# Two transformer layers in one kernel: router logits bank by bank, the last feed-forward's weights combined after the first expert's matmuls, the second attention's head rows gathered into one contraction, its last two matmul layers one bank apart

## The reference, cut to what matters

```
1 attention   16 heads of 64, causal, q/k/v from wq wk wv, output projection wo
2 mixture     8 experts, top 2 of softmax(x @ router_w + router_b), capacity 640 tokens
              per expert; gelu(x @ w1 + b1) @ w2 + b2, weighted sum
3 attention   16 heads of 8 with rotary positions, causal, scores equal to 0 masked too,
              output @ wo.T
4 feed-forward  h = x @ (w_fc as -1/0/1 times its scale).T + gate * x @ v.T @ fast_b.T @ u.T
              y = relu(h)^2 @ (w_proj as -1/0/1 times its scale).T
```

## Time and profile before

| | us |
|---|---|
| median of 3 runs | 1240.81 |
| lowest and highest of them | 1238.11, 1241.08 |
| the profiled execution's own time | 1239.13 |
| its span in the profile | 1237.3 |
| PE busy in the span | 1121.1 (91%) |
| PE weight loads, DVE, ACT, POOL busy | 851.2, 862.2, 815.4, 349.4 |
| mean granted TensorE clock | 0.958 of full |

### The profile page before, as it was taken

How to read it: one execution, slowest core, us unless ns; L and a number is a source line. 1 busy time by engine, 2 the same in 40 slices (tenths; PEclk the granted TensorE clock), 3 DMA queues, 4 the chain that set the end, 5 groups by cost and what they waited for, 6 DMA issues and landing times.

```text
span 1237.3 us, 28186 instructions
## 1 busy us (share of the span) xinstructions
PE 1121.1 (91%) x10202; PEld 851.2 (69%) x10202; DVE 862.2 (70%) x2486; ACT 815.4 (66%) x1915; POOL 349.4 (28%) x345
## 2 busy tenths in 40 slices
PE   5999999999999999999899976987888888888886
PEld 3787878787888787888576653665566556556674
DVE  6656566565656565645334547999999899999863
ACT  3766666767666666631233434998889889989932
POOL 1974646455464646213001202000000000000043
PEclk8999999999999999999599995998999899999998
DMA  6222223222322323211011043020310202110001
GB/s 161 59 69 76 69 58 77 63 59 64 80 54 70 76 59 75 65 36 34 15 35 43 25 97 46 2 40 27 66 31 10 40 6 36 26 15 2 2 1 34
DMA packets 33627, 58.90 MB, mean 48 GB/s; under 512 B 4906, under 2 KB 18114, under 8 KB 33490
## 3 DMA queue, kind: packets, MB, share of 16 engines
q1 hardware_dynamic: 32690, 55.52, 19.9%
q10 hardware_dynamic: 800, 1.57, 0.4%
HBM read 27.59 MB, written 4.33 MB: 26 GB/s over the span
## 4 chain that ended last, share of the span: by engine, by line
PE 56%; DVE 18%; issue 11%; ACT 7%; POOL 5%; DMA 2%; SPq 1%; ACTq 0%; POOLq 0%; DVEq 0%
PE pT L1278 12%; PE pO L1201 12%; PE pS L1239 10%; DVE Zb L956 9%; PE pS L1352 4%; ACT probs L719 3%; PE pT L1149 3%; PE pT L1365 3%; DVE Sm L971 3%; PE pS L1313 2%; PE pT L1153 2%; PE pS L1430 1%; ACT PT L699 1%; PE pS L1410 1%; DMA KS<-split 1%
## 5 line engine op out<-in xcount | busy, mean ns | idle before, releaser
L1278 PE MATMUL pT<-cst,probs 128*128 128x128 f32 x2304 | 369.9, 287 | 53.4 <-ACT probs L719 49.2
L1278 PEld LDWEIGHTS pT<-cst,probs 128*128 128x128 f32 x2304 | 257.0, 143 | 149.0 <-ACT probs L719 99.7
L719 ACT ACTIVATE probs<-probs,nmax 128x128 f32<-128x128 f32 (+7 forms) x256 | 198.7, 776 | 129.9 <-DVE nmax L966 128.9
L699 ACT COPY PT<-pT 128x512 f32<-128x512 f32 (+3 forms) x576 | 263.9, 482 | 16.8 <-PE pT L1278 15.6
L966 DVE CUSTOM_DVE_ANT_0 probs<-pS,causal_wide 128x128 f32<-128x128 f32 (+7 forms) x256 | 192.0, 750 | 91.2 <-PE pS L1239 83.6
L719 ACT ACTIVATE probs<-Sm,nmax 128x128 f32<-128x128 f32 (+7 forms) x256 | 199.6, 780 | 55.4 <-DVE nmax L971 49.1
L1201 PE MATMUL pO<-PT,V 128*64 128x128 f32 (+1 forms) x4608 | 233.5, 281 | 2.5 <-DVE attnT L925 1.1
L956 DVE TENSOR_SCALAR Zb<-pS 128x128 bf16<-128x128 f32 (+7 forms) x256 | 192.7, 753 | 20.0 <-PE pS L1245 19.4
L1201 PEld LDWEIGHTS pO<-PT,V 128*64 128x64 f32 (+1 forms) x4608 | 180.9, 114 | 36.3 <-issue 21.0
L971 DVE CUSTOM_DVE_ANT_0 Sm<-pS,Zb 128x128 f32<-128x128 f32 (+7 forms) x256 | 193.3, 755 | 4.5
L543 POOL TENSOR_TENSOR rstd<-rstd,power 128x4 f32<-128x4 f32 x32 | 32.6, 1019 | 552.4 <-DVE rstd L824 552.4
(11 more groups left out here) (189 smaller groups left out, 1370.2 us busy)
## 6 DMA issues: line engine op xcount, KB each, us to landing
wq_t<-factors SPq DMA_DIRECT2D x32, 256.0 KB, 4.0
Qs<-Ql SPq DMA_DIRECT2D x30, 256.0 KB, 3.7
Kh<-Kh SPq DMA_DIRECT2D x30, 256.0 KB, 3.4
Kl<-Kl SPq DMA_DIRECT2D x30, 256.0 KB, 4.6
QS<-split SPq DMA_DIRECT2D x72, 64.0 KB
KS<-split SPq DMA_DIRECT2D x72, 64.0 KB
w1s<-in_w SPq DMA_DIRECT2D x16, 128.0 KB, 2.3
w2s<-in_w SPq DMA_DIRECT2D x16, 128.0 KB, 2.2
```

Of the source, the lines that this page charges most:

```text
L699: nc.scalar.copy(PT[:, g % 2, h, k0 * P:(k0 + nk) * P], pT[r % TBANKS][:, 0:nk * P])\
L719: nc.scalar.activation(probs[:, i % NPROB, 0:n], src[:, 0:n], ACT.Exp, bias=nmax[:, i % 4:i % 4 + 1], scale=-1.0, accum_out=total).then_in ...
L1278: m = nc.tensor.transpose(pT[r % TBANKS][:, kt * P:(kt + 1) * P], probs[:, item % NPROB, (k0 + kt) * P:(k0 + kt + 1) * P], ident)
```

## The change

- In the stretch before the router the weight combination is gone. PE goes through the banks: transposes of bank j, then the logit matmuls of bank j-1 behind the copy of that bank alone.
- The weight combination stands behind `up(0)` and ahead of the rank counts, in banks 7 and 6, and ACT's three copies stand behind the first expert's gelus. PE waits for the last two of these copies ahead of the ninth transpose of the router weights.
- SP gathers the four heads of each half of the second attention by four transfers (8 partitions x 4 KB, SBUF to SBUF) into `compact[P, B, S]`, where head n lies on partitions 8n to 8n+7. The gather of half i stands behind the stacks of half i+2 in SP's order, and the last two behind the loop; each waits until its half's outputs are written. The output projection is one contraction per tile, and PE waits for a batch's 16 transfers ahead of that batch's first tile. `wo1s` is the plain transposed weight.
- The fourth sublayer's normalised input has a buffer of its own, `xn3`, since `compact` lies where `xn` was.
- In the last layers PE does bank j's upper matmuls ahead of bank j-1's projection.

The buffers, and SP's gathers:

```diff
-        wo1s = at(130, "wo1s", [P, G1, D])
+        wo1s = at(130, "wo1s", [P, D])
+        compact = at(148, "compact", [P, B, S])
+        xn3 = at(64, "xn3", [P, NT, D])
...
+            def gather(half):
+                b, g = divmod(half, G1)
+                sp.wait_ge(A[1]["n"], (half + 1) * ST)
+                for h in range(HPG):
+                    row = (g * HPG + h) * DH1
+                    sp.dma_start(compact[row:row + DH1, b, :], attn1T[h * (P // HPG):h * (P // HPG) + DH1, b, g, :])\
+                        .then_inc(ld_compact[b], 16)
...
                 if half == 2:
                     store(2)
                     store(3)
+                gather(half - 2)
+            gather(G1 * B - 2)
+            gather(G1 * B - 1)
```

On ScalarE, and on TensorE ahead of the router and behind `up(0)`:

```diff
-            act.wait_ge(lowA_done, 1)
-            nc.scalar.activation(lowA[:, :], bank[4][0:RANK, 0:D], ACT.Copy, scale=gates[:, 0:1]).then_inc(lowA_ready, 1)
-            act.wait_ge(w1e_done, 1)
-            nc.scalar.copy(w1e[:, :], bank[5]).then_inc(we_ready, 1)
-            act.wait_ge(w2e_done, 1)
-            nc.scalar.copy(w2e[:, :, :], bank[6]).then_inc(we_ready, 1)
             copies_T(1)
...
             gelus(0)
+            act.wait_ge(lowA_done, 1)
+            nc.scalar.activation(lowA[:, :], bank[7][0:RANK, 0:D], ACT.Copy, scale=gates[:, 0:1]).then_inc(lowA_ready, 1)
+            act.wait_ge(w2e_done, 1)
+            nc.scalar.copy(w2e[:, :, :], bank[6]).then_inc(we_ready, 1)
+            act.wait_ge(w1e_done, 1)
+            nc.scalar.copy(w1e[:, :], bank[7]).then_inc(we_ready, 1)
...
-            nc.tensor.matmul(bank[4][0:RANK, 0:D], fbs[:, :], vs[:, :], start=True, stop=True).then_inc(lowA_done, 1)
...
-            m.then_inc(w1e_done, 1)
-            pe.wait_ge(we_ready, 2)
-            transposes(1)
             pe.wait_ge(zeros_ready, 3)
-            pe.wait_ge(xnT_ready[1], NB)
-            for n in range(NT):
-                nc.tensor.matmul(bank[4][:, n * E:(n + 1) * E], xnT[:, n * P:(n + 1) * P], rws[:, :],
-                                 start=(n == 0), stop=False, skip_group_check=True)
+            for j in range(NB + 1):
+                if j < NB:
+                    pe.wait_ge(xn_ready[1], j + 1)
+                    for t in range(TPB):
+                        i = nc.tensor.transpose(bank[4 + j][:, t * P:(t + 1) * P], xn[:, j * TPB + t, :], ident)
+                    i.then_inc(tr_done[1], 1)
+                if j >= 1:
+                    pe.wait_ge(xnT_ready[1], j)
+                    for n in range((j - 1) * TPB, j * TPB):
+                        nc.tensor.matmul(bank[4][:, n * E:(n + 1) * E], xnT[:, n * P:(n + 1) * P], rws[:, :],
+                                         start=(n == 0), stop=False, skip_group_check=True)
...
             up(0)
+            nc.tensor.matmul(bank[7][0:RANK, 0:D], fbs[:, :], vs[:, :], start=True, stop=True).then_inc(lowA_done, 1)
+            pe.wait_ge(q_p, 5 * (FC1 + 1))
+            for f in range(FC1):
+                m = nc.tensor.transpose(bank[6][:, f * P:(f + 1) * P], wpj[:, f * P:(f + 1) * P], ident)
+            m.then_inc(w2e_done, 1)
+            pe.wait_ge(lowA_ready, 1)
+            for f in range(FC1):
+                nc.tensor.matmul(bank[7][:, f * P:(f + 1) * P], lowA[:, :], uTs[:, f * P:(f + 1) * P], start=True, stop=False)
+                m = nc.tensor.matmul(bank[7][:, f * P:(f + 1) * P], wfc[:, f, :], ident, start=False, stop=True)
+            m.then_inc(w1e_done, 1)
             pe.wait_ge(r_, 8 + NT)
...
             for n in range(NT):
+                if n == 2 * TPB:
+                    pe.wait_ge(we_ready, 2)
                 m = nc.tensor.transpose(bank[4 + n // TPB][0:E, (n % TPB) * P:(n % TPB + 1) * P], wgt[:, n, :], ident)
```

On TensorE in the second attention's output projection and the last layers:

```diff
             for n in range(NT):
-                for g in range(G1):
-                    m = nc.tensor.matmul(bank[n // TPB][:, (n % TPB) * P:(n % TPB + 1) * P],
-                                         attn1T[:, n // ST, g, (n % ST) * P:(n % ST + 1) * P], wo1s[:, g, :],
-                                         start=(g == 0), stop=(g == G1 - 1))
+                if n % ST == 0:
+                    pe.wait_ge(ld_compact[n // ST], 16 * HEADS)
+                m = nc.tensor.matmul(bank[n // TPB][:, (n % TPB) * P:(n % TPB + 1) * P],
+                                     compact[:, n // ST, (n % ST) * P:(n % ST + 1) * P], wo1s[:, :], start=True, stop=True)
...
                     m.then_inc(tr_done[3], 1)
+                    pe.wait_ge(xnT_ready[3], j + 1)
+                    for f in range(FC1):
+                        u = j * FC1 + f
+                        if u >= 2:
+                            pe.wait_ge(relu_ready, u - 1)
+                        nc.tensor.matmul(bank[6 + f % 2], w1e[:, f * P:(f + 1) * P], xnT[:, j * BANK:(j + 1) * BANK],
+                                         start=True, stop=True).then_inc(fc_done, 1)
                 if j >= 1:
                     pe.wait_ge(sq_ready, j * FC1)
...
-                if j < NB:
-                    pe.wait_ge(xnT_ready[3], j + 1)
...
```

More of the change, by code:

```diff
@@ L342, in build @@
         ld_stack = [sem("ld_stack0"), sem("ld_stack1")]
+        ld_compact = [sem("ld_compact0"), sem("ld_compact1")]
         lg_done = sem("lg_done")
@@ L473, in _ @@
             sp.wait_ge(y_done[1], NB)
-            sp.dma_start(wo1s[:, :, :], wo1).then_inc(ld_wo1, 16)
+            sp.dma_start(wo1s[:, :], wo1).then_inc(ld_wo1, 16)
             sp.wait_ge(tr_done[1], NB)
@@ L850, in norm_stage @@
                     if what == "x norm":
-                        norm(k, 1, j, lambda n: X[:, n, :], lambda n: xn[:, n, :], xn_ready[k])
+                        to = xn3 if k == 3 else xn
+                        norm(k, 1, j, lambda n: X[:, n, :], lambda n: to[:, n, :], xn_ready[k])
             def y_tile(n):
@@ L1322, in _ @@
                 pe.wait_ge(A[0]["cp_" + e2], L[0].copied[e2])
-            nc.tensor.matmul(bank[4][0:RANK, 0:D], fbs[:, :], vs[:, :], start=True, stop=True).then_inc(lowA_done, 1)
[L1324 to L1331, removed]
-            m.then_inc(w1e_done, 1)
-            pe.wait_ge(we_ready, 2)
-            transposes(1)
-            pe.wait_ge(zeros_ready, 3)
-            pe.wait_ge(xnT_ready[1], NB)
-            for n in range(NT):
-                nc.tensor.matmul(bank[4][:, n * E:(n + 1) * E], xnT[:, n * P:(n + 1) * P], rws[:, :],
-                                 start=(n == 0), stop=False, skip_group_check=True)
+            pe.wait_ge(zeros_ready, 3)
+            for j in range(NB + 1):
[9 more added lines that the diff above has]
+                                         start=(n == 0), stop=False, skip_group_check=True)
             nc.tensor.matmul(bank[4][:, 0:NT * E], onesf[:, :], rbs[:, :].rearrange("o (n e) -> o n e", n=1).to_broadcast([1, NT, E]),
@@ L1422, in _ @@
                     for t in range(TPB):
-                        m = nc.tensor.transpose(bank[4 + j % 2][:, t * P:(t + 1) * P], xn[:, j * TPB + t, :], ident)
+                        m = nc.tensor.transpose(bank[4 + j % 2][:, t * P:(t + 1) * P], xn3[:, j * TPB + t, :], ident)
                     m.then_inc(tr_done[3], 1)
+                    pe.wait_ge(xnT_ready[3], j + 1)
[5 more added lines that the diff above has]
+                                         start=True, stop=True).then_inc(fc_done, 1)
                 if j >= 1:
@@ L1432, in _ @@
                     m.then_inc(y_done[4], 1)
-                if j < NB:
-                    pe.wait_ge(xnT_ready[3], j + 1)
[L1435 to L1438, removed]
-                        nc.tensor.matmul(bank[6 + f % 2], w1e[:, f * P:(f + 1) * P], xnT[:, j * BANK:(j + 1) * BANK],
-                                         start=True, stop=True).then_inc(fc_done, 1)
 def kernel(L0_attn_x, L0_attn_wq, L0_attn_wk, L0_attn_wv, L0_attn_wo, L0_ffn_router_w, L0_ffn_router_b, L0_ffn_w1,
@@ L1454 @@
     wl1 = np.stack([qkv[0], qkv[0][:, swap], qkv[1], qkv[1][:, swap], qkv[2]]).reshape(5, D, D).transpose(2, 0, 1)
-    wo1 = np.zeros((HPG, P // HPG, G1, D), np.asarray(L1_attn_wo).dtype)
-    wo1[:, 0:DH1] = np.asarray(L1_attn_wo).T.reshape(G1, HPG, DH1, D).transpose(1, 2, 0, 3)
     arrays = {
```

2 lines of the change are left out of this document (1 added, 1 removed).

## The result

| | before | after |
|---|---|---|
| median of 4 runs each, us | 1239.46 (1237.72 to 1241.08) | 1226.50 (1225.86 to 1227.89) |
| profiled execution, its span | 1239.13, 1237.3 | 1227.89, 1226.1 |
| PE busy | 1121.1 | 1103.0 |
| mean granted clock | 0.958 | 0.961 |

The ratio is 0.990 (95% interval 0.988 to 0.992), a gain clear of the noise though small. The forecast of 1232.0 had the sign and the two places right; the time lies under the low end of the range, 1228.

What follows compares the result with a forecast made beforehand. The kernel was taken as a row of stages with separate limits, its last-ending chain more than half PE. Router 2.4 plus tail 6.4 made 8.8 us, taking 1240.8 to 1232.0; overall range 1228 to 1237.

Steps and rivals of the forecast that it cites:

- logits by bank: Before the router: logits follow each bank's copy, so DVE starts the router at 587.7, 3.6 us earlier.
- rank counts behind the combination: Router: the counts wait for the moved combination on PE, losing 1.2 us of the 3.6 gained.
- router weights and b2: Router, 602.03 to 612.65: assumed to keep its 10.6 us, so no gain.
- start of up(1) to the first down: Start of the experts: instructions unchanged, so no gain counted.
- stages that don't change, second attention above all: First attention, experts, second attention: same instructions, so they only shift; no gain counted.
- tail: After the second attention: last statistics 7.8 us earlier, less 1.4 for a low clock, leaving 6.4 us.
- Part 1: Before the router: combination moved away and logits done bank by bank; DVE starts at 587.7, 3.6 us earlier.
- Part 2: Combination behind up(0), ending 598.3 at full clock: counts wait 1.2 us, leaving 2.4 us gained.
- Part 3 and 4: Gather with shorter projection, 2.73 us; last layers 8.6 us a bank instead of 9.3; together 7.8, or 6.4 with low clock.
- The rival that ends slower: Last layers: clock stays low after the wait at 1180 to 1184.9, 13.1 us a bank; total 1247; chance 5%.
- The rival on a better clock: No fall at 1184.9, counts undelayed, b2 products at 0.114: up to 14.9 us gained, 1225.9; chance 10%.
- they move as a block: First attention, experts and second attention keep their instructions, so they only shift in time; no gain counted.

Runs made afterwards that it cites:

- e2_tail: Kernel before with the change's gather, compact, xn3, plain wo1s and last-layer order, router as before; 1231.70 us, ratio 0.9947.
- e4_early: Changed kernel with the weight combination put back ahead of the banked transposes and logits; 1228.66 us, ratio 0.9931.
- e3: Kernel before with only the new order of the last layers, bank j's upper matmuls ahead of bank j-1's projection; 1235.89 us, ratio 0.9990.
- e11_att: e9_fillAB with the first score product doubled for items of up to three key tiles in the second attention; 1225.77 us.
- e12_before: Kernel before, unchanged, profiled again; 1240.70 us in one run.
- e16_after: Changed kernel, unchanged, profiled again; 1224.65 us in one run.
- e7_fill: Changed kernel with useless matmuls in three PE waits: five before the router's last xn, ten before the second attention, five before the last layers' first xn; 1226.35 us.
- e9_fillAB: Changed kernel with useless matmuls in two PE waits: five before the router's last xn, five before the last layers' first xn; 1225.06 us.
- e13_fill3: e9_fillAB with three more useless matmuls before the weight combination's second half; 1225.28 us.
- e8_gather: Kernel before with gather, compact, xn3 and the single contraction, last layers in the old order, router as before; 1234.29 us, ratio 0.9958.

## Why the prediction was right or wrong

By terms, forecast against the means of the profiles (tail and unchanged stages: four of each kernel; router: seven with the old code, five with the new):

| term | forecast | measured |
|---|---|---|
| logits by bank | 3.6 | 3.4 (18.0 to 14.66) |
| rank counts behind the combination | -1.2 | -0.5 (0 to -0.9) |
| router weights and b2 | 0 | 1.2 (8.4 to 7.25); 3.0 in the first pair |
| start of up(1) to the first down | 0 | -0.2 |
| stages that don't change, second attention above all | 0 | 2.0, not told from chance |
| tail | 6.4 | 6.2; 5.6 in the first pair |
| sum | 8.8 | 12.1 |

**Right.** Part 1: DVE was forecast at 587.7 and came at 588.43 in a profile in which everything before it was alike. The 16 instructions behind the last xn took 0.21 each, not the 0.182 I took. Part 2: the combination's end, 598.3, came at 598.38, the rank counts at 598.22 for 598.4, the router weights at 599.20 for 599.6; the clock there was full. The closeness is in part luck: up(0) began 0.7 us late and took 5.64 us instead of 6.19. And the wait of 1.2 us that I charged to the counts was about 0.1 here (10.77 from the logits to the router weights, 10.69 before) and 0.5 in the mean of five. Part 3 and 4: banks 8.49 apart for 8.6; no wait for squares; the last two projections in one; in the last layers the clock is low in the first transposes and upper matmuls only. The landing of the gather was forecast 3.7 us after the last output and took 4.7, because the issue takes 0.62 each and not the 0.34 I put in; I had PE through at 1180 with nothing more to do before 1184.9; in e2_tail PE waited 2.29 us and the tail (48.0) was no longer than in the four profiles of after.

**The rival that ends slower** did not come. The Trainium skill (TensorE: Matmul & The Clock Gate, "HAM oscillation") tells of a kernel in which each wait between bursts, a DMA wait of about 3 to 5 us, throttles PE anew. My step from it to every bank here was too wide, since the waits between the banks are shorter than that kernel's. The trace: behind waits of 1.91 and 0.68 us the clock is 1.00 from 1190 to 1200, and behind the idle 4.81 us it was low, which agrees. But in before a wait of 1.92 us was followed by a low clock, so the length of a wait alone doesn't decide.

**Wrong.** The step that failed is the sentence "Router weights and b2 (602.03 to 612.65) I leave at the 10.6 us". It took the time of one execution at 0.50 for the price of the code. Before itself takes 7.4 to 7.6 there in three of its four profiles. The term of nothing was 3.0 us in the first pair and 1.2 in the means; without the two profiles at 10.63 it is 0.3 (7.5 to 7.25). The rival on a better clock named this very piece (32 of 0.22 at 0.114), gave it 10%, and tied it to the change; e4_early and the old router code in e2 and e3 are as fast with the combination in its old place.

The second failure is in "they move as a block". The second attention keeps its instructions on PE, DVE and ACT, but not its time: 421.2 to 427.1 over 17 profiles with the same matmuls there (all but e11_att). It took 4.4 us less in the first pair and 2.1 less in the mean of four, with ranges that overlap (423.8 to 427.0 against 421.2 to 426.4). Windows of before, of e12_before and of e16_after over the same part of it:

```profile
974.00:984.00 10.00, 9.10 (x56) 5.25 (x57) 7.67 (x30) 7.42 (x25) 0.00 (x0) 0.56 0.55 69
```

```profile
974.00:984.00 10.00, 9.54 (x59) 5.87 (x59) 7.47 (x27) 7.76 (x26) 0.00 (x0) 0.51 0.55 69
```

```profile
971.00:981.00 10.00, 8.39 (x92) 5.08 (x85) 9.86 (x33) 8.93 (x28) 0.00 (x0) 1.00 0.56 67
```

PE is busy in all three and DVE, which leads here, does 9.86 us of work at clock 1.00 and 7.5 to 7.7 at the low one. The time follows the clock: over the 13 profiles without matmuls of no use, the attention takes 421.2 to 427.0 us with 29.5 to 50.7 us of it at the low clock (correlation 0.96, 0.27 us for each us). The gathers on SP show no effect on it: 424.0 us in the mean of the seven profiles with them, 424.3 in the six without. Whether the new router code, which shifts all that follows, makes such falls rarer is open: 423.0 in the six with it (421.2 to 426.4), 425.1 in the seven without (423.0 to 427.0). But e7_fill, e9_fillAB and e13_fill3 have it too, at 427.0, 425.8 and 427.1.

The third is the base. I subtracted from the median of 3 runs, 1240.8; 67 runs give 1238.75. Of the 5.4 us between 1232.0 and 1226.6, this is 2.0, router 1.5, second attention and the other unchanged stages 2.0, less 0.2 for the tail. A smaller miss is the rank counts' wait, 1.2 us forecast and 0.5 measured; it is in the router's 1.5. The range took the spread of three runs for that of the kernel, and no term at all for the draws of unchanged stages; these are 3 us in the router stretch, 1.5 in the experts and 6 in the second attention. With half of the last alone its low end is 1225.

## What to carry to other kernels

Where a stretch of the profile runs at about half the granted clock with PE busy, its duration may be one draw and not the price of the code: take a second execution before such a row enters a sum, and put the difference into the range, for the unchanged stages too. Moving work out of the way of a late bank wins what stands behind the last arrival (here 16 of 32 small matmuls), not what is taken away. Where a bank's steps on one engine wait for another engine, let the neighbouring bank's work fill the wait. A transfer added in front cost nothing here, since it landed before the engine that leads needed its bank.

## What the runs showed of the hardware that I had not expected

- The same program takes 1231.9 to 1243.4 us, and whole stretches take one of a few lengths (7.4 to 7.6 or 10.63; 105.5 or 107.0), with the granted clock at 1.2 or 2.4 GHz over the same instructions.
- PE may be busy throughout and still stay at 0.50: 6 us in e8_gather (604 to 610), in transposes of the router weights and products with 8 rows.
- A transfer from 8 partitions to 8 others took 0.62 us of issue on SP, a stack transfer, also of 8 partitions, 0.30; the last of four landed 4.7 us after the start of the last output.
- Over 63 runs of one program the duration rises by 0.27 us for each us spent at the low clock, not by the half that would be lost if PE set the pace throughout.
- Idle PE time filled with matmuls of no use brought the clock to 1.00 in both places, worth 2.2 us at the logits and 1.0 to 2.0 in the tail (47.0 to 48.0 against a mean of 48.95), of which the times show at most 1.6.
